# Residual low-rank FFN over a gated LoRA layer: V and half of W laid side by side, one load per chunk, and two steps moved

## The reference, cut to what matters

```python
base   = einsum('btd,od->bto', x, W)                      # W 1024 x 1024, x 2048 tokens x 1024, all fp32
logits = einsum('btd,ed->bte', x, Wr) + 5 * one_hot(id)   # 8 experts
gates  = softmax over the top 2 of logits, 0 elsewhere
h      = einsum('btd,erd->bter', x, A)                    # 8 experts x rank 16
y      = base + 2 * einsum('bter,bte,eor->bto', h, gates, B)
out    = x + einsum('bti,oi->bto', y, (U * S) @ V.T)      # U, V 1024 x 256
```

## Time and profile before

| | |
|---|---|
| median of three runs | 163.91 us (163.9 to 164.58) |
| the profiled execution, own time | 163.66 us |
| its span | 161.7 us |
| PE busy | 155.2 us, 96% of the span |
| DVE, ACT, POOL busy | 82.1, 56.4, 39.6 us |
| bytes moved by DMA | 32.70 MB, mean 202 GB/s |
| loads of W (15 of 256 KB), of V (8 of 128 KB), issue to landing | median 5.9 and 5.6 us |

### The profile page before, as it was taken

One profiled execution on the slowest core, in us unless ns is written; L12 is line 12 of the kernel. 1 busy time (PEld: TensorE's weight loads), 2 busy tenths in 40 slices (PEclk: granted clock), 3 DMA queues, 4 the chain that ended last, 5 costly groups with the idle time before them and its releaser, 6 DMA issues.

```text
span 161.7 us, 2481 instructions
## 1 busy us (share of the span) xinstructions
PE 155.2 (96%) x900; PEld 143.1 (89%) x900; DVE 82.1 (51%) x260; ACT 56.4 (35%) x132; POOL 39.6 (24%) x31
## 2 busy tenths in 40 slices
PE   7689999999999999999999999999999999999992
PEld 4589999999898989898999999898989898989882
DVE  0569679246855271726263534445362627180843
ACT  5557684328234142323323140404131313111210
POOL 2000013060552350505050505051414233200000
PEclk9999999999999999999999999999999999999999
DMA  4899999996020658292938283846573430303045
GB/s 128 256 349 397 396 404 404 411 410 240 23 108 0 202 192 305 97 323 99 287 135 305 113 286 131 263 147 244 166 223 134 130 130 0 130 4 130 0 195 196
DMA packets 11676, 32.70 MB, mean 202 GB/s; under 512 B 1553, under 2 KB 3089, under 8 KB 11537
## 3 DMA queue, kind: packets, MB, share of 16 engines
q1 hardware_dynamic: 11664, 32.55, 56.8%
HBM read 24.16 MB, written 8.39 MB: 201 GB/s over the span
## 4 chain that ended last, share of the span: by engine, by line
PE 80%; SPq 7%; DMA 6%; ACT 3%; DVE 2%; issue 1%
PE pj L249 15%; PE pj L251 15%; PE pj L250 15%; PE fin L249 10%; PE fin L251 10%; PE fin L250 10%; DMA w_raw<-in_W 6%; SPq L169 3%; SPq L172 2%; PE zt L308 2%; DVE w_lo L488 2%; ACT xT_hi L432 1%; PE gt L296 1%; ACT us_hi L435 1%; PE zt L251 1%
## 5 line engine op out<-in xcount | busy, mean ns | idle before, releaser
L242 POOL TENSOR_TENSOR xT_lo<-xt_raw,xT_hi 128x1024 fp32r<-128x1024 f32 x16 | 38.4, 2403 | 98.1 <-ACT xT_hi L432 98.1
L249 PE MATMUL pj<-proj_hi,xT_hi 128*128 128x392 f32 x128 | 45.0, 352 | 0.0
L251 PE MATMUL pj<-proj_hi,xT_lo 128*128 128x392 f32 x128 | 43.6, 341 | 0.0
L250 PE MATMUL pj<-proj_lo,xT_hi 128*128 128x392 f32 x128 | 43.4, 339 | 0.0
L249 PE MATMUL fin<-us_hi,zT_hi 128*128 128x512 f32 (+1 forms) x66 | 27.0, 409 | 0.0
L250 PE MATMUL fin<-us_lo,zT_hi 128*128 128x512 f32 (+1 forms) x66 | 25.6, 388 | 0.0
L251 PE MATMUL fin<-us_hi,zT_lo 128*128 128x512 f32 (+1 forms) x66 | 25.6, 388 | 0.0
L249 PEld LDWEIGHTS pj<-proj_hi,xT_hi 128*128 128x128 f32 x128 | 24.0, 188 | 1.1
L250 PEld LDWEIGHTS pj<-proj_lo,xT_hi 128*128 128x128 f32 x128 | 24.1, 188 | 0.6
L251 PEld LDWEIGHTS pj<-proj_hi,xT_lo 128*128 128x128 f32 x128 | 24.0, 188 | 0.0
L510 DVE SCALAR_TENSOR_TENSOR logit<-target,pj 128x8 f32<-128x8 f32 x16 | 2.6, 163 | 41.9 <-PE pj L251 41.9
(11 more groups left out here) (69 smaller groups left out, 183.1 us busy)
## 6 DMA issues: line engine op xcount, KB each, us to landing
xt_raw<-in_xt SPq DMA_DIRECT2D x16, 512.0 KB, 4.3
x_all<-in_x SPq DMA_DIRECT2D x16, 512.0 KB, 3.9
out<-x_all SPq DMA_DIRECT2D x14, 512.0 KB, 2.9
w_raw<-in_W SPq DMA_DIRECT2D x15, 256.0 KB, 5.9
v_raw<-in_V SPq DMA_DIRECT2D x8, 128.0 KB, 5.6
u_raw<-in_U SPq DMA_DIRECT2D x1, 1024.0 KB, 11.6
out<-x_all SPq DMA_DIRECT2D x3, 256.0 KB, 2.2
aw_raw<-in_AW SPq DMA_DIRECT2D x1, 544.0 KB, 6.8
```

What stands on the lines that cost most here:

```text
L242: nc.gpsimd.tensor_sub(xT_lo[:, t % 2, :, :], xt_raw[:, t % XTR, :, :], xT_hi[:, t % 2, :, :].bitcast(F32)).then_inc(xt_lo, 1)
L249: nc.tensor.matmul(dst, l_hi, r_hi, start=first, stop=False, skip_group_check=shared)
L250: nc.tensor.matmul(dst, l_hi, r_lo, start=False, stop=False, skip_group_check=shared)
L251: return nc.tensor.matmul(dst, l_lo, r_hi, start=False, stop=last, skip_group_check=shared)
```

## The change

Three edits. (1) The host lays chunk k of V (256 columns) and chunk k of the first half of W (512 columns) side by side, 3 KB per partition, each chunk contiguous in memory; the second half of W is laid out by chunks too. SP issues one load where it issued two, eight loads fewer in all. Chunk 0 comes in two pieces: V's 256 columns with W's first 128, then W's other 384. (2) DVE makes the low part of B behind P's second half and ahead of the targets, no longer behind chunk 14. (3) In `step(2)` tile 1's gated h is transposed behind the sixth projection instead of the fifth.

```diff
-            load_v(0)
-            sp.dma_start(w_raw[:, 0, 0:P], W_v[:, 0, 0:P]).then_inc(w_load[0], 16)
-            sp.dma_start(w_raw[:, 0, P:HQ], W_v[:, 0, P:HQ]).then_inc(w_rest_load, 16)
+            first = RANK + P
+            sp.dma_start(vw_raw[:, 0, 0:first], VW[0, :, 0:first]).then_inc(vw_load[0], 16)
+            sp.dma_start(vw_raw[:, 0, first:], VW[0, :, first:]).then_inc(vw_rest_load, 16)
             for k in range(1, OC):
-                load_v(k)
-                load_w(k)
-            load_w(OC)
-            load_w(OC + 1)
+                sp.dma_start(vw_raw[:, k, :], VW[k, :, :]).then_inc(vw_load[k], 16)
+            load_w(0)
+            load_w(1)
...
-            step(2, gh_at=4, mix_at=DC - 1, z_after=0)
+            step(2, gh_at=5, mix_at=DC - 1, z_after=0)
...
             def split_v(k):
-                act.wait_ge(v_load[k], 16)
-                nc.scalar.copy(v_hi[:, k, :], v_raw[:, k, :]).then_inc(v_hi_done, 1)
+                act.wait_ge(vw_load[k], 16)
+                nc.scalar.copy(v_hi[:, k, :], vw_raw[:, k, 0:RANK]).then_inc(v_hi_done, 1)
...
-                if i == OC + 6:
-                    dve.wait_ge(b_hi_done, 1)
-                    nc.vector.tensor_sub(b_lo[:, :, :], b_raw[:, :, :], b_hi[:, :, :].bitcast(F32)).then_inc(b_lo_done, 1)
             split_p(2)
             split_p(3)
+            dve.wait_ge(b_hi_done, 1)
+            nc.vector.tensor_sub(b_lo[:, :, :], b_raw[:, :, :], b_hi[:, :, :].bitcast(F32)).then_inc(b_lo_done, 1)
...
+        "VW": np.concatenate([V.reshape(P, OC, RANK), W[:, :, :D // 2]], axis=2).transpose(1, 0, 2),
+        "W": W[:, :, D // 2:].transpose(1, 0, 2),
...
-        "V": V,
```

More of the change, by code:

```diff
@@ L14, with adaln_ffn @@
 SCALING = 32.0 / 16.0
-def adaln_ffn(nc, xt, x, ids, W, AW, B, U, S, V, out):
+def adaln_ffn(nc, xt, x, ids, VW, W, AW, B, U, S, out):
     P = 128
@@ L23, in adaln_ffn @@
     R = ER // E
-    O, RANK = V.shape
-    OC = O // P
+    OC, _, HQ = W.shape
+    O = OC * P
+    RANK = U.shape[1] * P
     MC = RANK // P
@@ L32, in adaln_ffn @@
     COLS = ER + E + RANK
-    HQ = D // 2
     MH = HQ // P
@@ L40, in adaln_ffn @@
     assert ER == P and O == D and DC == 2 * MH and RANK * 2 == BANK and COLS <= BANK
-    W_v = W.rearrange("(p k) d -> p k d", k=OC)
-    V_v = V.rearrange("(p k) r -> p k r", k=OC)
     x_v = x.rearrange("(g p) d -> g p d", p=P)
@@ L60, in adaln_ffn @@
         xT_lo = sb("xT_lo", [P, 2, DC, P], F32R)
-        w_raw = sb("w_raw", [P, 2 * OC, HQ], F32)
+        vw_raw = sb("vw_raw", [P, OC, RANK + HQ], F32)
+        w_raw = sb("w_raw", [P, OC, HQ], F32)
         w_hi = sb("w_hi", [P, WRING, HQ], F32R)
         w_lo = sb("w_lo", [P, WRING, HQ], F32R)
-        v_raw = sb("v_raw", [P, OC, RANK], F32)
         v_hi = sb("v_hi", [P, OC, RANK], F32R)
@@ L106, in adaln_ffn @@
         bv_ps = zt[:, RANK:2 * RANK]
-        w_load = [sem(f"w_load{i}") for i in range(2 * OC)]
-        w_rest_load = sem("w_rest_load")
-        v_load = [sem(f"v_load{k}") for k in range(OC)]
+        vw_load = [sem(f"vw_load{k}") for k in range(OC)]
+        vw_rest_load = sem("vw_rest_load")
+        w_load = [sem(f"w_load{k}") for k in range(OC)]
         aw_load = sem("aw_load")
@@ L160, in fin_bank, with w_chunk @@
             return fin[i % FINS]
+        def w_chunk(i):
+            return vw_raw[:, i, RANK:RANK + HQ] if i < OC else w_raw[:, i - OC, :]
         block = ctx.enter_context(nc.Block())
@@ L166, in _, with load_w @@
         def _(sp):
[L167 to L172, removed]
+            def load_w(k):
+                sp.dma_start(w_raw[:, k, :], W[k, :, :]).then_inc(w_load[k], 16)
             def load_xt(t):
@@ L408, in split_w @@
                 h, k = divmod(i, OC)
-                act.wait_ge(w_load[i], 16)
                 if i == 0:
-                    nc.scalar.copy(w_hi[:, 0, 0:P], w_raw[:, 0, 0:P]).then_inc(w_hi_done, 1)
-                    act.wait_ge(w_rest_load, 16)
-                    nc.scalar.copy(w_hi[:, 0, P:HQ], w_raw[:, 0, P:HQ]).then_inc(w_hi_done, 1)
+                    nc.scalar.copy(w_hi[:, 0, 0:P], w_chunk(0)[:, 0:P]).then_inc(w_hi_done, 1)
+                    act.wait_ge(vw_rest_load, 16)
+                    nc.scalar.copy(w_hi[:, 0, P:HQ], w_chunk(0)[:, P:HQ]).then_inc(w_hi_done, 1)
                     return
+                if i >= OC:
+                    act.wait_ge(w_load[i - OC], 16)
                 if i >= WRING:
                     act.wait_ge(w_used, i - WRING + 1)
-                nc.scalar.copy(w_hi[:, i % WRING, :], w_raw[:, i, :]).then_inc(w_hi_done, 1)
+                nc.scalar.copy(w_hi[:, i % WRING, :], w_chunk(i)).then_inc(w_hi_done, 1)
             def split_v(k):
-                act.wait_ge(v_load[k], 16)
-                nc.scalar.copy(v_hi[:, k, :], v_raw[:, k, :]).then_inc(v_hi_done, 1)
+                act.wait_ge(vw_load[k], 16)
+                nc.scalar.copy(v_hi[:, k, :], vw_raw[:, k, 0:RANK]).then_inc(v_hi_done, 1)
             def split_p(b):
@@ L487, in split_w @@
                 dve.wait_ge(w_hi_done, i + 2)
-                nc.vector.tensor_sub(w_lo[:, i % WRING, :], w_raw[:, i, :],
+                nc.vector.tensor_sub(w_lo[:, i % WRING, :], w_chunk(i),
                                      w_hi[:, i % WRING, :].bitcast(F32)).then_inc(w_lo_done, 1)
@@ L492, in split_v @@
                 dve.wait_ge(v_hi_done, k + 1)
-                nc.vector.tensor_sub(v_lo[:, k, :], v_raw[:, k, :], v_hi[:, k, :].bitcast(F32)).then_inc(v_lo_done, 1)
+                nc.vector.tensor_sub(v_lo[:, k, :], vw_raw[:, k, 0:RANK], v_hi[:, k, :].bitcast(F32)).then_inc(v_lo_done, 1)
             def split_p(b):
@@ L640 @@
     O, RANK = V.shape
+    OC = O // P
+    W = np.asarray(inputs["L0_cond_W"]).reshape(P, OC, D)
     x2 = x.reshape(NB * SEQ, D)
@@ L645 @@
         "ids": np.repeat(np.asarray(inputs["itok_B_0_7"]), SEQ).reshape(TILES, P).T,
-        "W": inputs["L0_cond_W"],
+        "VW": np.concatenate([V.reshape(P, OC, RANK), W[:, :, :D // 2]], axis=2).transpose(1, 0, 2),
+        "W": W[:, :, D // 2:].transpose(1, 0, 2),
         "AW": np.concatenate([A.reshape(E * R, D).T, Wr.T], axis=1).reshape(DC, P, E * R + E).transpose(1, 0, 2),
```

6 lines of the change are left out of this document (3 added, 3 removed).

## The result

The changed kernel took 163.49 us (median of 20 runs) beside 164.08 us (20 runs) of the kernel before; the ratio is 0.9964, 95% interval 0.9946 to 0.9981. Two of the changed kernel's 20 runs, 165.36 and 193.4 us, fell in a slower state of the chip and are left out of the ratio. That is a gain of 0.6 us where 1.7 were forecast, and less than the 0.8 us that I had set as telling from no change. The profiled execution took 163.38 us, 0.28 less than before's.

A forecast was written before the change was run, and what follows sets the result against it. PE was taken as the bound, its early stalls caused by late loads; joined loads gain 1.75 us, rounded to 1.7, the other edits 0. Span 161.7 + 2.0 less 1.7 is 161.96, plus 0.25 gives 162.2 us; range 161.3 to 163.6.

The forecast's parts named there:

- What bounds the kernel: Whole kernel: PE, busy 155.2 of 161.7 us, bounds it; only its early stalls for late loads can shrink.
- in between, 5.4 and 7.9: Early loads: chunk 1 lands at 5.4 us and chunk 3 at 7.9, between the 260 and 397 GB/s cases.
- PE reaches chunk 3 at 10.2: PE's early path: chunk 1 starts at 7.2, chunk 3 at 10.2 instead of 11.68, a gain of 1.5 us.
- The two terms of the landing: Landing of W's chunk 12: 0.96 us of idle time plus 0.90 of 1.80 us slow time saved, 1.9 us earlier.
- The rule for the time of a load: Loads: 2.0 us plus bytes at 436 GB/s, an estimated 2.9 us for a lone 393 KB load.
- Cost 0: B's low part in its new place, 32.99 to 34.2 us: delays nothing, with 1.0 us of slack before `make_bv`.
- the targets behind it are done at 34.7: DVE behind B's low part: targets take 0.5 us, end at 34.7, before its next operation at 35.45.
- The later transpose: `step(2)`: one projection later is 0.54 us, `ghT_lo` ends at 47.63, 0.28 in time for `mix`; cost 0, no gain.
- Whatever earlier start chunk 13 gets, the end gets: From chunk 13 to the end: PE stays the bound, so chunk 13's gain, 1.75 us, reaches the end.
- The port rival: `make_bv`: POOL takes the port before B's low part, PE waits 1.55 us, time 163.75 us; chance 0.08.
- The slow stretch stays: Loads, 2 to 10 us: the start makes engines slow, chunk 12 lands only 0.6 us earlier, 163.3 us; chance 0.12.
- The chance of 0.75: Whole kernel: chance of faster, from the forecast case at 0.62 and PE going straight on at 0.13.

The follow-up runs named there:

- d1: Changed kernel with targets and B's low part ahead of P's second half, mix of tile 0 behind the sixth projection; 162.37 us, 0.9867 of before.
- d3: d2 with the joined loads of chunks 1 and 2 issued by ScalarE at its start; 163.93 us, 0.9955 of before.
- a1: Joined loads alone: changed kernel with B's low part back behind chunk 14 and the transpose behind the fifth projection; 162.95 us, 0.9927 of before.
- a3: Changed kernel with the cast of the ids and the targets ahead of P's second half; 162.61 us, 0.9929 of before.
- a4: Changed kernel with the targets behind P's second half but ahead of B's low part; 164.71 us, 1.0043 of before.
- c2: Changed kernel with V's and W's joined rows kept partition by partition (strided), one load per chunk; 163.55 us, 0.9968 of before.
- d2: d1 with three more matmuls of zeros between chunk 0 and chunk 1, where PE waits; 162.26 us, 0.9890 of before.
- b1: Kernel before with only tile 1's gated h transposed behind the sixth projection instead of the fifth; 164.58 us, 1.0006 of before.
- a2: Kernel before with only B's low part moved behind P's second half; 164.46 us, 1.0010 of before.
- c1: Kernel before with every chunk of V and W contiguous in memory, still two loads per chunk; 164.40 us, 0.9999 of before.
- e2: Changed kernel with chunks 1 to 7 in one load each but cut into 1 KB pieces per partition; 163.91 us, 0.9992 of before.
- e1: Changed kernel with x's tiles 0 and 1 loaded ahead of V and W; 165.19 us in its one execution.

## Why the prediction was wrong

**What bounds the kernel** held: PE's stalls, and nothing behind chunk 13 but a shift, save for two places, the mix of tile 0 and the end.

**The loads: landings put at even distances.** The step that failed is "in between, 5.4 and 7.9". It spreads the landings evenly, so that chunk 2 lands at about 6.7, in time for PE, and the sum then goes from chunk 1 straight to "PE reaches chunk 3 at 10.2". In the changed kernel chunk 2 landed at 7.92 and started at 7.92 + 1.71 = 9.63; PE, done with chunk 1, could have taken it at 7.15 + 1.54 = 8.69. So it came 0.94 us late, chunk 3 started at 11.16 and not at 10.2, and chunk 13 came 1.0 us earlier, not 1.75. It is no single case: in the other profiles with joined 3 KB loads, d1 and d3 aside, chunk 2 landed between 7.45 and 8.10 and started between 9.16 and 9.81.

That chunk 1 came at 5.44 and 7.15, as forecast (5.4 and 7.2), was luck: 5.44 is the earliest of seven profiles with this load, the others have 5.68 to 6.23. It also bought nothing, as chunk 2 bounds PE in each. The two terms of the landing came out smaller than I had them: of the 0.96 us idle time 0.64 went (the share is 0.96 and not 1), and of the 1.80 us of slow time 0.73, where I took 0.90; 1.4 us together, not 1.9. Chunk 12 was copied at 20.10, 1.7 us earlier, but this too differs between executions of one load order: 21.49 in a1, 20.50 in a3 and a4, 20.56 in c2, 19.91 in d2.

The size of the gain is read from several profiles: in the changed kernel, c2, a3 and a1, `make_bv` starts at 34.18, 34.11, 33.88 and 34.87, 34.26 in the mean, against 35.18 and 35.34 in before and b1: 1.0 us. (a4 waits there for B; a2, c1 and d1 had the slow pitch of matmuls early on, see the end.) These are few, and a1's landings were late. But the times bear the gain out: a1 and a3, which have it without the loss at the mix, took 0.9927 and 0.9929 of before's time, 1.2 us less, with intervals from 0.6 to 1.8 us. The profiles' 1.0, less 0.35 at the end (below), lies at the low end of these.

Why the second joined load lands 1.6 to 2.5 us behind the first, when the engines bring a chunk a us soon after, is open. In d1, of the same loads, it landed at most 0.95 us behind; in e2 0.99. In d3, which issues both 0.9 us earlier, both are there before ACT asks for them (5.93, 6.76), at chunk 0's cost. The rule for the time of a load that the prediction quotes stands in the Trainium skill ("DMA: Bandwidth & Descriptors", in "Anatomy of one DMA") as a fit for loads issued by GpSimd. These are issued by SP, and the trace doesn't agree: chunk 1 as one load of 393 KB, with others in flight beside it, landed 3.8 us behind its issue (1.65 to 5.44), where the estimate was 2.9.

**B's low part: "Cost 0".** The subtraction itself cost nothing, and POOL was held for it as said. What failed is the sentence that the targets behind it are done at 34.7: I moved them by 1.2 us, into POOL's `xT_lo`, and weighed the port for the moved instruction alone, not for those that it pushes along. The first that met a running `xT_lo` was the cast of the ids. It was held for 2.2 us, the first gates came 1.3 us later against PE, and 0.5 us reached PE at the mix of tile 0 and stayed to its last matmul (the table's last column). a2 makes the loss by the move alone, a3 takes it away by moving the targets alone: shown. Of the 1.3 us only so much arrives because the way there is ACT's: its exponential waits for the gates, and its `bv_hi` (L475) behind it starts at 37.80, 3.62 us behind `make_bv`'s start, where before it was 3.08 (38.26 - 35.18): 0.54 later, and `ghT_hi` and `ghT_lo` follow it.

**The later transpose** cost nothing, as said.

**The end.** PE's last matmul starts at 157.93 instead of 158.43, 0.50 earlier, but the span is only 0.15 shorter. From there to the end it takes 3.57 us instead of 3.22. "Whatever earlier start chunk 13 gets, the end gets" failed here too, for a reason that isn't known. The last bytes move about 2.1 us behind the start of the last matmul in both kernels; the difference lies behind them. The last two windows of before, then of the changed kernel (the last column is GB/s):

```profile
160.50:160.60 0.10, 0.00 (x0) 0.00 (x0) 0.00 (x0) 0.00 (x0) 0.00 (x0) 1.00 0.09 21
160.60:161.65 1.05, 0.00 (x0) 0.00 (x0) 0.00 (x0) 0.00 (x0) 0.00 (x0) 1.00 0.00 0
```

```profile
160.00:160.10 0.10, 0.00 (x0) 0.00 (x0) 0.00 (x0) 0.00 (x0) 0.00 (x0) 1.00 0.09 21
160.10:161.50 1.40, 0.00 (x0) 0.00 (x0) 0.00 (x0) 0.00 (x0) 0.00 (x0) 0.55 0.00 0
```

So of 1.75 us forecast the profile has 1.00 from the loads, less 0.52 at the mix, less 0.35 at the end, 0.15 in the span; the medians say 0.6.

**The rivals.** The port rival had the right resource and the right price but the wrong victim; a4 shows it in the form in which it was put. "The slow stretch stays" gave nearly the right time, 163.3, and the port case another, 163.75; both by luck, since the stretch did speed up and B's low part did keep the port. The measured time lies in the stated range only because the range took in the first of them. The chance of 0.75 for faster by 0.5% was too high, since it left out the cast behind B's low part, which I had not looked at. Without that neighbour, in a1 and a3, the kernel is faster by 0.7%.

## What to carry to other kernels

When a long VectorE step is moved, list what stands behind it and ask of each whether it now runs while GpSimd reads SBUF; a 0.2 us cast can become 2.4 us. When a sum of waits is shifted, follow every chunk in turn, and where two loads follow each other closely, look whether their landings do so too before spreading them evenly: the stall goes to the first chunk that isn't ready. Fewer and larger loads raised the rate at the start from 260 to 277 GB/s to 299 to 348; by the running rate the size of the pieces has a part in it, by the times number and size are not told apart. Contiguity in memory brought nothing that the median shows.

## What the runs showed of the hardware

**A small cast is held too.** The cast from int32 to fp32 of 128 x 16 took 0.17 us alone and 2.37 us behind a running `xT_lo` (changed kernel, a2). It has one SBUF input. The Trainium skill ("SBUF — State Buffer", who interferes with whom) says that casts can enter a two-port mode and then contend with GpSimd, and that the order of issue decides who is blocked. The traces agree in one order: behind a running `xT_lo` the cast was held to its end in all five kernels that have it there (changed, a2, c2, e1, e2), and 0.17 us is the time of a cast with `xT_lo` not yet started. The other order is seen with B's low part alone, a subtraction with two SBUF inputs: 1.22 us ahead of `xT_lo`, which then took 3.19 instead of 2.46 us, and 3.30 behind it.

**TensorE's clock fell early in some executions.** PE was idle ahead of chunk 1 for 2.47 us in a2 (6.54 to 9.01) and for 1.74 in d1 (6.20 to 7.94), and the granted clock was low afterwards. Windows of a2 and of d1 (granted clock behind POOL's column):

```profile
9.00:15.00 6.00, 5.99 (x28) 5.99 (x29) 4.38 (x9) 3.77 (x9) 0.00 (x0) 0.50 1.06 394
```

```profile
8.00:12.00 4.00, 4.00 (x21) 4.00 (x22) 3.86 (x9) 3.29 (x8) 0.00 (x0) 0.57 1.02 395
```

0.50 is the lower level, 1.2 of 2.4 GHz, and the matmuls of a chunk then follow each other at 0.21 us instead of 0.12, so chunks take 2.6 us and not 1.44. With its longer wait (9.01 against 8.00) that is a2's 2.5 us. The kernel before, idle from 6.56 to 8.00, kept the upper level, 1.00. So did a3 behind a wait nearly as long as d1's:

```profile
7.63 0.39 PE L245 MATMUL fin<-v_hi,w_hi 128*128 128x256 f32 x1 [1.66 <-DVE w_lo L485]
```

And c1, idle there for only 1.13 us, has the slow pitch of 0.21 from chunk 0 on, until 13.8 us, though its granted clock reads 1.00. So a long early wait and a low clock went together in a2 and d1, but that the wait is the cause isn't shown. What it costs shows in the times: a3's three executions with a mean granted clock of 0.987 to 0.988 took 164.26 to 164.64 us, its nine with 0.996 and more 162.41 to 163.09. One of d1's seven was low (0.989, 163.74 us), of d2's six, with the wait filled, none; that is too few to call the filling shown.

**The end differs by kernel.** From the start of the last matmul to the span's end it is 3.21 to 3.23 us in before, a2, b1, c1 and d3, and 3.55 to 3.62 in the changed kernel, a1, a3, a4, c2, e1, e2, d1 and d2. The first four issue 8 loads more on SP; d3, with two fewer still, has the short end too. The cause is open, and no run was made for it.
